# Last batch of a fused adaLN block: low-rank rows signalled block by block, high terms first, last addition and store in pieces

## What is computed

```python
def _L0_ffn_ref(x, U1, V1, U2, V2, b1, b2):
    P = jnp.einsum('bsh,hr->bsr', x, U1)          # 1024 -> rank 256
    H = jnp.einsum('bsr,rf->bsf', P, V1) + b1     # 256 -> 2 * 2752
    gate, up = (H[..., :INTER], H[..., INTER:])
    act = jax.nn.silu(gate) * up
    Z = jnp.einsum('bsi,ir->bsr', act, U2)        # 2752 -> rank 256
    out = jnp.einsum('bsr,rh->bsh', Z, V2) + b2   # 256 -> 1024
    return out
...
x = x + ga * _L0_attn_ref(h, ...)
h = _layernorm(x, axis=-1) * (1 + cb) + sb
x = x + gb * _L0_ffn_ref(h, ...)
```

## Time and profile before

| | |
|---|---|
| device time, three executions | median 1199.25 us (1198.07 to 1199.92) |
| profiled execution | 1196.55 us, its span 1194.7 us |
| TensorE busy | 1143.3 us, 96% of the span |
| VectorE, ScalarE, GpSimd busy | 49%, 41%, 33% of the span |
| chain that ended last | PE 84%, DMA 4%, DVE 4%, ACT 3% |
| mean granted TensorE clock | 0.994 of full speed |

### The profile page before, as it was taken

How to read it: one execution, slowest core, us unless ns; L and a number is a source line. 1 busy time by engine, 2 the same in 40 slices (tenths; PEclk the granted TensorE clock), 3 DMA queues, 4 the chain that set the end, 5 groups by cost and what they waited for, 6 DMA issues and landing times.

```text
span 1194.7 us, 15376 instructions
## 1 busy us (share of the span) xinstructions
PE 1143.3 (96%) x5882; PEld 943.0 (79%) x5882; DVE 587.0 (49%) x937; ACT 491.4 (41%) x787; POOL 390.5 (33%) x339
## 2 busy tenths in 40 slices
PE   5588999999999999999999999999999999999998
PEld 5357898887778788888888888888888888888886
DVE  1557687786665334434444344443543434344343
ACT  0037577676777543224224323323322432332241
POOL 1007899891112657313031130211303113021110
PEclk9899999999999999999999999999999999999999
DMA  9984998857553642421040150122113015013001
GB/s 358 360 311 149 339 343 302 310 190 271 212 211 129 199 143 79 163 85 71 28 149 3 69 176 1 71 90 87 71 50 127 23 48 176 1 71 122 20 1 70
DMA packets 57197, 169.61 MB, mean 142 GB/s; under 512 B 6176, under 2 KB 10784, under 8 KB 55072
## 3 DMA queue, kind: packets, MB, share of 16 engines
q1 hardware_dynamic: 57120, 168.57, 39.4%
HBM read 126.51 MB, written 42.04 MB: 141 GB/s over the span
## 4 chain that ended last, share of the span: by engine, by line
PE 84%; DMA 4%; DVE 4%; ACT 3%; issue 2%; SPq 1%; POOL 1%; DVEq 0%; ACTq 0%
PE bank L537 23%; PE bank L538 23%; PE bank L539 23%; PE bank L702 6%; PE bank L597 4%; PE bank L576 2%; DMA mask_a<-in_mask 2%; ACT nrm L957 2%; PE bank L688 1%; DMA pt_dram<-pt_st 1%; DVE h_lo L1316 1%; DMA wm_sb<-in_wmod 1%; DVE bn L1183 1%; PE bank L877 1%; SPq L377 1%
## 5 line engine op out<-in xcount | busy, mean ns | idle before, releaser
L1121 ACT ACTIVATE act<-bank,b_sb 128x512 f32<-128x512 f32 (+1 forms) x176 | 121.3, 690 | 497.3 <-PE bank L539 481.4
L1448 DVE SCALAR_TENSOR_TENSOR act<-bank,b_sb,act 128x512 f32<-128x512 f32 (+1 forms) x176 | 131.9, 750 | 376.2 <-PE bank L539 352.8
L537 PE MATMUL bank<-pt,v_hi 128*128 128x512 f32 x688 | 268.8, 391 | 1.3 <-DVE act L1448 1.3
L538 PE MATMUL bank<-pt,v_hi 128*128 128x512 f32 x688 | 267.7, 389 | 0.0
L539 PE MATMUL bank<-pt,v_lo 128*128 128x512 f32 x688 | 267.7, 389 | 0.0
L1599 POOL TENSOR_TENSOR x2t<-gbb_bc,x2t 128x512 f32<-128x512 f32 x64 | 85.4, 1357 | 250.8 <-DMA x2t<-x_dram 250.8
L1458 DVE TENSOR_TENSOR act_lo<-act,act_hi 128x512 fp32r<-128x512 f32 (+1 forms) x176 | 160.5, 912 | 0.9
L537 PEld LDWEIGHTS bank<-pt,v_hi 128*128 128x128 f32 x688 | 129.1, 188 | 31.7 <-DVE act L1448 4.3
L539 PEld LDWEIGHTS bank<-pt,v_lo 128*128 128x128 f32 x688 | 129.2, 188 | 27.1
L538 PEld LDWEIGHTS bank<-pt,v_hi 128*128 128x128 f32 x688 | 129.2, 188 | 26.1
L537 PE MATMUL bank<-act_hi,u_hi 128*128 128x512 f32 x336 | 130.9, 390 | 0.7 <-DVE act_lo L1458 0.6
(11 more groups left out here) (134 smaller groups left out, 1670.0 us busy)
## 6 DMA issues: line engine op xcount, KB each, us to landing
wm_sb<-in_wmod SPq DMA_DIRECT2D x9, 2048.0 KB, 10.3
xs<-in_x SPq DMA_DIRECT2D x32, 512.0 KB, 5.6
x_dram<-xs SPq DMA_DIRECT2D x32, 512.0 KB, 5.1
xs<-x_dram SPq DMA_DIRECT2D x32, 512.0 KB, 5.5
x2t<-x_dram SPq DMA_DIRECT2D x32, 512.0 KB, 4.1
out<-x2t SPq DMA_DIRECT2D x32, 512.0 KB, 4.9
pt_dram<-pt_st SPq DMA_DIRECT2D x8, 1024.0 KB, 7.5
pt<-pt_dram SPq DMA_DIRECT2D x8, 1024.0 KB, 5.7
```

Source lines behind the costliest of these rows:

```text
L537: nc.tensor.matmul(acc, s_hi, m_hi, start=start, stop=False)
L538: nc.tensor.matmul(acc, s_hi, m_lo, start=False, stop=False)
L1121: nc.scalar.activation(act[0:w, j % 2, :], bank[0:w, j % 2, :], ACT.Silu, bias=b1_sb[0:w, i, 0:1]).then_inc(silu_done, 1)
L1448: nc.vector.scalar_tensor_tensor(act[0:w, j % 2, :], up, b1_sb[0:w, i, 1:2], act[0:w, j % 2, :], ALU.add, ALU.mult).then_inc(act_done, 1)
```

## The change

In the last batch alone, four things change:

- `z_product` increments a new semaphore, `z_first`, at the last matmul of r = 0 in its last call. ScalarE's first copy waits for `z_first`, its second for `z_step`.
- `out_product` waits for `z_hi` and `z_lo` block by block, inside output m = 0.
- The last addition (m = 7) becomes two of 256 columns, each with its own increment of `out_ready`.
- The last tile's store becomes three DMAs: columns 0 to 511 (256 KB), 512 to 767 and 768 to 1023 (128 KB each).

In all eight batches, the six matmuls of an output change their order: the four with z_hi first, for r = 0 and r = 1, and the two with z_lo behind them.

```diff
@@ SyncE, batch()
                 for n in range(TT):
+                    if last and n == TT - 1:
+                        for k, (a, e) in enumerate(((0, HALF), (HALF, HALF + HALF // 2), (HALF + HALF // 2, D))):
+                            sp.wait_ge(out_ready, b * 8 + 2 * n + 1 + k)
+                            sp.dma_start(out_tiles[b, n][:, a:e], x2t[:, n, a:e]).then_inc(out_stored, 16)
+                        continue
                     sp.wait_ge(out_ready, b * 8 + 2 * n + 2)
...
-            sp.wait_ge(out_stored, 64 * NB)
+            sp.wait_ge(out_stored, 64 * NB + 32)
@@ TensorE, z_product()
+                        if b == NB - 1 and j == IB - 1 and r < RB - 1:
+                            last.then_inc(z_first, 1)
@@ TensorE, out_product()
-                pe.wait_ge(z_lo_ready, b * 2 + 2)
+                early = isinstance(b, int) and b == NB - 1
+                if not early:
+                    pe.wait_ge(z_lo_ready, b * 2 + 2)
                 pe.wait_ge(v2_lo_ready, b * 4 + 4)
...
                     for r in range(RB):
-                        last = three(bank[:, 6 + m % 2, :], z_hi[:, r, toks], z_lo[:, r, toks],
-                                     v2_hi[:, r, cols], v2_lo[:, r, cols], r == 0, r == RB - 1)
+                        if early and m == 0:
+                            pe.wait_ge(z_hi_ready, b * 2 + 1 + r)
+                        nc.tensor.matmul(bank[:, 6 + m % 2, :], z_hi[:, r, toks], v2_hi[:, r, cols],
+                                         start=r == 0, stop=False)
+                        nc.tensor.matmul(bank[:, 6 + m % 2, :], z_hi[:, r, toks], v2_lo[:, r, cols],
+                                         start=False, stop=False)
+                    for r in range(RB):
+                        if early and m == 0:
+                            pe.wait_ge(z_lo_ready, b * 2 + 1 + r)
+                        last = nc.tensor.matmul(bank[:, 6 + m % 2, :], z_lo[:, r, toks], v2_hi[:, r, cols],
+                                                start=False, stop=r == RB - 1)
                     last.then_inc(o_mm, 1)
@@ ScalarE, batch()
-                ae.wait_ge(z_step, b * IB + IB)
+                if last:
+                    ae.wait_ge(z_first, 1)
+                else:
+                    ae.wait_ge(z_step, b * IB + IB)
                 if not at_start(b):
                     ae.wait_ge(o_mm, b * 8)
                 for r in range(RB):
+                    if last and r == RB - 1:
+                        ae.wait_ge(z_step, b * IB + IB)
                     nc.scalar.activation(z_hi[:, r, :], bank[:, 4 + r, :], ACT.Copy).then_inc(z_hi_ready, 1)
@@ VectorE, batch()
-                    nc.vector.tensor_tensor(half, bank[:, 6 + m % 2, :], half, ALU.add).then_inc(out_ready, 1)
+                    if last and m == TT * NH - 1:
+                        for c in range(0, HALF, HALF // 2):
+                            piece = x2t[:, n, h * HALF + c:h * HALF + c + HALF // 2]
+                            nc.vector.tensor_tensor(piece, bank[:, 6 + m % 2, c:c + HALF // 2], piece,
+                                                    ALU.add).then_inc(out_ready, 1)
+                    else:
+                        nc.vector.tensor_tensor(half, bank[:, 6 + m % 2, :], half, ALU.add).then_inc(out_ready, 1)
```

More of the change, by code:

```diff
@@ L215, in adaln_block @@
         z_step = sem("z_step")
+        z_first = sem("z_first")
         z_hi_ready = sem("z_hi_ready")
```

## The result

The changed kernel takes 1194.96 us (median of seven executions, 1193.13 to 1196.72), the kernel before 1199.25 us (seven, 1197.06 to 1200.06). The ratio is 0.9967, with a 95% interval of 0.9956 to 0.9978: 2.6 to 5.3 us less. The profiled execution took 1194.4 us with a span of 1192.6, against 1196.55 and 1194.7. Here is the first thing to explain: the two traces are 2.1 us apart, the medians 4.3.

The account below looks back on a forecast made before the run. TensorE, busy 96% of the span, was taken as the bound, leaving its idle hole and the tail; 1.79 + 0.85 = 2.64 us off 1199.25 gave 1196.6 us, range 1195.3 to 1198.6.

Parts of the forecast that it names:

- The median of the runs lies 2.70 above the profiled execution: Whole program: the difference between median and profiled execution was taken as untouched by the change, giving 1199.25 - 2.64 = 1196.6.
- The start of the output: Last batch, between Z's last matmul and the output matmuls: block 0 starts early, gaining 1.79 us, bounds 1.4 to 2.00.
- The stall of 0.20 at the third matmul: Last batch, output m = 0: the third matmul waits for z_hi of block 1 and ends at 1178.91 instead of 1178.71.
- The upper bound of 2.00: Start of the last batch's output: gain of 2.00 us if late weight loads, pulled ahead of matmuls in flight, cost nothing.
- The order of the matmuls: All eight batches, six matmuls per output: same matmul and weight load counts, so a gain of zero.
- The last addition: End of the last batch, addition in two pieces: piece two ends 0.75 after the start, 0.06 us later than before.
- The last store: End of the program, store in three: 0.95 us saved in data less 0.10 later issue, net 0.85 us; bounds 0.3 to 0.85.
- the data time of 128 KB: Last store: a quarter of 512 KB's 1.28 us, 0.32 us, if rows of 1 KB keep the rate.
- The 1.3 us for other things: Last store: of the 2.6 us to landing of 512 KB, 1.3 us are not data.
- The rival with a landing of 2.1: Last store: the short store lands near the short read's 2.1 us, tail gains 0.3, total 2.1, time 1197.15; chance 0.23.
- a rule on small transfers: Last store: the skill says to join many small transfers, since small ones are mostly overhead; its constant was not followed.
- The upper end of the range: Whole program: 1198.6 us, from the weak early start and a few ns a matmul, with half the spread.

Follow-up runs that it names:

- e2: Kernel before with only the new order of the six matmuls of every output, in all eight batches; 1198.16 us, ratio 0.9997.
- e3: Kernel before with the early start alone (first-block signal, waits by block, new order in the last batch only), last addition and store whole; 1195.17 us, ratio 0.9973.
- e4: Kernel before with the tail alone: last addition in two, last store in three; 1197.49 us, ratio 0.9992.
- e6: Kernel before with the first-block signal alone: ScalarE's first copy waits for z_first, TensorE keeps its order and waits; 1197.83 us, ratio 0.9991.
- e7: Kernel before with waits block by block and high terms first, but without z_first; 1197.18 us, ratio 0.9986.
- e9: Kernel before with four more ScalarE copies ahead of the first z_hi, lengthening TensorE's empty hole; 1201.98 us, ratio 1.0029.
- e10: Kernel before with the same four more ScalarE copies and 16 unread matmuls filling TensorE's hole; 1199.84 us, ratio 1.0015.
- e1: The changed kernel timed again, unaltered, beside the kernel before; 1196.22 us, ratio 0.9974.

## Why the prediction was wrong

The prediction's working of the path held to 0.3 us in all, and its largest error there, in the tail, pointed the other way: the path gained less than forecast, while the median moved more. What failed is the step from the path to the median: "The median of the runs lies 2.70 above the profiled execution; nothing in the change touches that difference." Part of that difference is a clock that falls behind the hole, at 1.58 us a time, and the change does take it away.

- **The start of the output: right.** 1.79 us forecast, 1.76 measured; m = 0 ended 1.91 after Z's end, forecast 1.88. The stall of 0.20 at the third matmul was 0.17 (0.40 instead of 0.23). The first start cost 0.09 more than at once, which the working had left out. The upper bound of 2.00, by which the pulled-ahead weight loads would hide the wait, was not reached: the load that needs z_hi of block 1 started at 1178.68, 0.10 before the second matmul ended, and the third still ended 0.40 after the second.
- **The order of the matmuls: right.** Zero; e2 gives 0.9997, and in the trace after lines 905, 907 and 912 take 391, 389 and 389 ns on the mean, forecast 390.
- **The last addition: right** to 0.01 us.
- **The last store: the term was too large.** 0.85 us forecast, 0.60 measured. The issue came 0.12 later instead of 0.10, and from there to the end of the span it was 0.72 shorter instead of 0.95. The term that was too small is the data time of 128 KB, 0.32 us "if rows of 1 KB keep the rate": they took about 0.5. The 1.3 us for other things held. 512, 256 and 128 KB land in 2.6, 2.0 and 1.8 to 1.9 us. The rival with a landing of 2.1 was too dark by 0.2 to 0.3. The prediction set a rule on small transfers against the cut (the Trainium skill, "DMA: Bandwidth & Descriptors", section "Rules for kernel authors"). That rule says "mostly overhead" of transfers under 64 KB, and both sizes here are larger.
- **What was missing: the clock.** "The whole hole but the change of instruction", 2.00 us, stood as the upper bound of the first part. It was none. The trace of before had the granted clock at 1.00 behind the hole, and I took that one execution as the rule. In about three executions in ten, with 14% to 60% by group, the hole costs another 1.58 us. The sum should have been 2.36 + 0.44 = 2.8, ratio 0.9977, and its upper bound 2.9 + 1.58 = 4.5.
- **The base of the sum.** With 2.8 us the median would still be 1196.5, not 1194.96. The same program gave medians of 1194.96 and 1196.22 in two groups, and before gave 1199.25 and 1198.3 to 1198.6. A median of few executions is uncertain by about 1 us here, on both sides of the difference. The range allowed 1 us of spread below its low end; with the clock's 1.58 as well it would have gone to 1193.8 and held the result. The clock alone, at 0.44 us on the mean, doesn't bring the forecast to the measured time: the larger part of the miss of 1.6 us is this uncertainty. The upper end of the range, 1198.6, doesn't follow from its own terms either (1197.2 + 1.2 + half of 1.85 is 1199.3); nothing hangs on it here.

Shown are the path (e3 with e4, and e6 with e7, add up to it within 0.1 us) and, from the traces, that the clock falls behind an idle TensorE and not behind a busy one on the same path (e9 against e10, one trace each; the counts of low clocks, 6 of 9 against 0 of 12, go the same way). That the rest of the first 4.3 us, some 1.5, is spread is likely but not shown: e1 came out at 2.3, and its interval still reaches 4.3. The reported clocks tie a part of the spread to the start of the program; of the seven executions of before in the first comparison no clock is on record. Which start an execution gets, and why the same hole is hit in one execution and not in another, stays open.

## What to carry to other kernels

Price an idle hole of TensorE with what follows it: beside its own length, the matmuls behind it can run at half clock for some 3.4 us (here 1.58 us lost), and one trace that shows full clock there does not exclude it. Look at the granted clock of every execution, not of one, and compare medians only where the mix of clocks is alike. When a product hands over between engines block by block, count which buffers the earlier work frees: interleaving gave 0.13 us of the path, and 0.57 once more PSUM banks broke the wait that took its place. Before a last store is cut, read its data time: the first cut gave 0.57 us, the second at most 0.1.

## What the runs showed of the hardware

After 2.0 us without a matmul the granted clock stood at half for 3.4 us in e2 and e4, but not in the trace of before, with the same hole; after 3.9 us it did in e9, and in e10, where the matmuls filled 3.66 of 4.0 us, it did not. At the end of the program a store of 128 KB to DRAM landed in 1.8 to 1.9 us, one of 256 KB in 2.0 and one of 512 KB in 2.6; about 1.3 us of each were not data. The two of 128 KB followed each other and were in flight together.
